# First stage without GpSimd: the initial state on ScalarE, the adding of x on VectorE, operations over two tiles, and a pipeline over pairs

## The chip, the cores and the metric

The kernel runs on one core of one Trainium2 chip. Its metric is the device time of a launch in microseconds. Before the change it is 1729.39 us, the median of 3 runs (1728.51 to 1730.09).

## The reference, cut to what matters

Two recurrent layers work on x of shape 64 x 128 x 512 (batch, time, features), each added to its input. The first is a gated linear recurrence that is written with cumulative sums, so all its time steps can be computed at once; the second is a GRU that goes step by step.

```python
# layer 0: h0 = cond (64, 512)
f  = sigmoid(x @ W_f.T + b_f);  i = sigmoid(x @ W_i.T + b_i)
s  = f + i + EPS
c  = x @ W_h.T + b_h
L  = cumsum(log(f / s + EPS), axis=time)
hidden = cumsum(exp(L_last - L_previous) * (i / s) * c) + exp(L) * h0
x1 = x + hidden
# layer 1: h = 0, video = cond
z = sigmoid(x1[t] @ W_z + h @ U_z + video @ C_z + b_z)
r = sigmoid(x1[t] @ W_r + h @ U_r + video @ C_r + b_r)
hh = tanh(x1[t] @ W + (r * h) @ U + video @ C + b)
h = (1 - z) * h + z * hh;   y[t] = x1[t] + h
```

## The kernel before, in words

The first stage (the span's first 634 us) computes x1, the second (the rest) runs the GRU. Features lie on the 128 partitions, in 4 blocks e.

First stage. The batch is cut into 16 chunks c of 4 rows; a chunk is 512 columns (4 rows x 128 time steps). A tile n is one block e of one chunk, 128 x 512; a pair q is two tiles, and a chunk has two pairs (h = 0 and 1). For each tile TensorE computes three groups (f, i, candidate) of 12 matmuls each (line 717), every group into one of the 8 PSUM banks. Both the weights and x are split into a high and a low part; for the chunk ahead ScalarE writes the high part of x into XS (x_hi, line 318) and VectorE the low one (x_lo, line 489). XS has two slots. The first group of a chunk needs the high part from its first matmul on and the low part from its ninth.

After TensorE, a tile goes back and forth between the engines: sigmoids on ScalarE (lines 344, 349), two gate operations on VectorE (439, 441), two logarithms on ScalarE (354, 355), four scans of 128 steps and an addition on VectorE (470, 475), exp(L) and four exponentials on ScalarE (361, 366), a product and a scan of 512 on VectorE (481, 485). GpSimd multiplies exp(L) with the initial state (826) and adds x (833), and VectorE adds both parts into x1c (459), laid out as (time block, e, time, row). The candidate is multiplied in by VectorE (448). ScalarE loads a table set twice in each pair (351, 369).

SyncE issues the DMAs from its queue. At the start of the pairs with h = 0 it waits until the whole chunk c - 1 is in x1c, stores it into a scratch in DRAM (line 246), and then loads x of chunk c + 1 into the raw buffer that chunk c - 1 has left (line 250). Between the pairs the weights of the second layer come into the buffers called stage; VectorE and ScalarE turn U into two float16 parts in small steps (u_step, 21 of them, and the scalings of line 377), and GpSimd takes three maxima over the partitions (837).

Each engine takes its instructions in the order of its own program; semaphores carry the dependencies. Lines 331 to 378 (ScalarE), 544 to 572 (VectorE), 816 to 837 (GpSimd), 694 to 719 (TensorE, with pair_order) and 241 to 263 (SyncE) set the order of the first stage.

Second stage. 128 steps; in each TensorE works through the recurrent matmuls (761, 773) and 18 projections of the next time block (741). GpSimd takes (1 - z) * h (849), y (860) and the low part of x1 (864), ScalarE its high part (413); the last three read x1 from the raw buffers through a rearranged view.

Of the kernel before, what the change touches and what calls it, by code (L numbers as in the profile page):

```python
# [9 lines left out]
ALU = mybir.AluOpType  # L10
# [21 lines left out]
def build(nc, x, cond, w1, b1, w2, u2, c2, b2, out):  # L32
    ctx = ExitStack()
    with ctx:
# [175 lines left out]
        def last_src(j):  # L210
            return x1c[1][:, j * 128:(j + 1) * 128].rearrange("p (e t b) -> p e t b", e=KT, t=TC)
# [7 lines left out]
        def _(sp):  # L219
# [21 lines left out]
            for q in range(NQ):  # L241
                c, h = divmod(q, 2)
                if h == 0 and c >= 1:

                    sp.wait_ge(s_x1, 4 * c)
                    sp.dma_start(x1d[:, :, c - 1, :].rearrange("j p n -> p j n"),
                                 x1c[(c - 1) % 2].rearrange("p (j n) -> p j n", j=NCH)).then_inc(d_x1d[(c - 1) % 2], 16)
                    if c + 1 < NCH:
                        sp.wait_ge(s_px, 4 * c)
                        sp.dma_start(raw[(c + 1) % 2], x[c + 1]).then_inc(d_x[(c + 1) % 2], 16)  # L250
                if q in (8, 15, 22):
                    g = (8, 15, 22).index(q)
# [13 lines left out]
            sp.wait_ge(s_x1, 4 * NCH)  # L266
# [4 lines left out]
            sp.wait_ge(s_px, 4 * NCH)  # L271
# [29 lines left out]
        def _(act):  # L301
# [29 lines left out]
            for q in range(NQ):  # L331
                c, h = divmod(q, 2)
                if q == NQ - 1:
                    early_hi(0)
                I, G = Ib[q % 2], Gb[q % 2]
                pair = (2 * q, 2 * q + 1)
                for n in pair:
# [561 lines left out]
```

## Time and profile before

| | us |
|---|---|
| median of 3 runs | 1729.39 |
| the profiled execution | 1729.3 |
| its span, first to last instruction | 1727.5 |
| TensorE busy | 1642.9 (95%) |
| VectorE busy | 1516.5 (88%) |
| ScalarE busy | 732.9 (42%) |
| GpSimd busy | 450.6 (26%) |

The mean granted clock of TensorE is 0.980 of full speed. 1.8 us of the profiled execution lie outside the span. The shares are means over both stages; from 700 us on TensorE shows no idle time in the windows, in the first stage it does.

### The profile page before, as it was taken

What the parts mean: (1) busy time and instruction counts of PE and PEld (TensorE: products, weight loads), DVE (VectorE), ACT (ScalarE), POOL (GpSimd) and SP (SyncE); (2) the same over time, 40 slices, a digit from 0 to 9 for tenths busy, and PEclk for the clock granted to TensorE, in tenths of its full rate; (3) what the DMA queues carried; (4) which work ended last, traced back from release to release, by engine and by line L of the source; (5) the groups of instructions that cost most, each with busy time, mean ns of one, the idle gap of its engine ahead of it and who ended that gap; (6) DMA issues with size and microseconds to landing.
All of it is one profiled execution on the core that took longest, in us unless ns stands there. A gap on an engine that the chain in (4) does not pass through costs nothing.

```text
span 1727.5 us, 43869 instructions
## 1 busy us (share of the span) xinstructions
PE 1642.9 (95%) x17918; PEld 1399.7 (81%) x17918; DVE 1516.5 (88%) x3472; ACT 732.9 (42%) x1642; POOL 450.6 (26%) x451
## 2 busy tenths in 40 slices
PE   9988998988999969999999999999999999999997
PEld 6877776767777758888888888888888888888996
DVE  6999989999999986888888888888888888888776
ACT  6656656666667651323322323323323323233222
POOL 1233222332233320222222212222222222222211
PEclk9999998998999989999999999999999999999999
DMA  5111212311211241011011010010010110100000
GB/s 174 50 49 49 73 50 69 102 49 50 73 49 49 74 167 50 2 50 51 2 50 51 2 51 28 25 50 17 36 51 2 51 50 2 51 27 2 27 28 27
DMA packets 45465, 82.51 MB, mean 48 GB/s; under 512 B 1616, under 2 KB 37712, under 8 KB 38480
## 3 DMA queue, kind: packets, MB, share of 16 engines
q1 hardware_dynamic: 45264, 79.71, 13.3%
q8 instruction: 141, 2.31, 0.5%
q14 instruction: 60, 0.49, 0.1%
HBM read 46.15 MB, written 33.55 MB: 46 GB/s over the span
## 4 chain that ended last, share of the span: by engine, by line
PE 65%; DVE 24%; issue 10%; ACT 1%; DMA 0%; DVEq 0%; SPq 0%; POOL 0%; ACTq 0%
PE ps L741 32%; PE ps L773 18%; PE ps L761 12%; DVE Lb L470 8%; DVE AR L481 4%; DVE AR L459 3%; PE ps L717 3%; DVE AR L448 3%; DVE AR L439 2%; DVE AR L485 1%; DVE XS L489 1%; DVE U L517 1%; DVE am L497 0%; DMA raw<-in_x 0%; DVE XS L523 0%
## 5 line engine op out<-in xcount | busy, mean ns | idle before, releaser
L741 PE MATMUL ps<-XS,W 128*128 128x512 f32 (+1 forms) x2448 | 592.6, 388 | 14.7 <-DVE XS L541 14.3
L717 PE MATMUL ps<-XS,W 128*128 128x512 f32 x2304 | 547.9, 400 | 55.9 <-ACT XS L318 49.8
L717 PEld LDWEIGHTS ps<-XS,W 128*128 128x128 f32 x2304 | 443.5, 194 | 160.0 <-issue 57.9
L741 PEld LDWEIGHTS ps<-XS,W 128*128 128x128 f32 x2448 | 426.6, 189 | 85.5 <-issue 15.0
L773 PE MATMUL ps<-HL,U 128*128 128x128 f16 (+1 forms) x4096 | 254.4, 216 | 0.0
L849 POOL TENSOR_TENSOR zc<-zc,Hst 128x256 f32<-128x256 f32 x128 | 94.8, 741 | 586.8 <-ACT zc L399 586.8
L773 PEld LDWEIGHTS ps<-HL,U 128*128 128x128 f16 x4096 | 219.8, 98 | 0.0
L397 ACT ACTIVATE prer<-prer 128x128 f32<-128x128 f32 x256 | 78.5, 310 | 309.4 <-DVE prer L616 270.5
L826 POOL TENSOR_TENSOR AR<-AR,CT 128x512 f32<-128x512 f32 x64 | 83.7, 1308 | 410.6 <-ACT AR L361 410.6
L761 PEld LDWEIGHTS ps<-HL,U 128*128 128x128 f16 x4608 | 152.2, 98 | 35.6 <-issue 34.8
L761 PE MATMUL ps<-HL,U 128*128 128x64 f16 x4608 | 174.8, 193 | 4.9 <-DVE HL L655 4.9
L399 ACT ACTIVATE zc<-prez 128x256 f32<-128x256 f32 x128 | 53.4, 417 | 265.9 <-DVE prez L616 240.0
L592 DVE TENSOR_TENSOR AR<-ps,V 128x512 f32<-128x512 f32 (+1 forms) x204 | 127.7, 652 | 22.8 <-PE ps L741 22.8
L470 DVE TENSOR_TENSOR_SCAN Lb<-AR 128x128 f32<-128x128 f32 x256 | 147.4, 637 | 0.0
L611 DVE SCALAR_TENSOR_TENSOR prer<-ps,du,AR 128x128 f32<-128x128 f32 x256 | 87.5, 347 | 61.0 <-PE ps L773 56.6
L773 PE MATMUL ps<-RL,U 128*128 128x128 f16 (+1 forms) x2048 | 128.7, 216 | 0.5 <-DVE RL L634 0.5
L407 ACT ACTIVATE hn<-Hst 128x256 f32<-128x256 f32 x128 | 53.6, 418 | 143.0 <-DVE Hst L661 143.0
L773 PEld LDWEIGHTS ps<-RL,U 128*128 128x128 f16 x2048 | 110.2, 98 | 1.5 <-DVE RL L634 0.6
L833 POOL TENSOR_TENSOR AR<-AR,raw 128x512 f32<-128x512 f32 x64 | 107.1, 1674 | 6.1 <-POOL AR L826 0.2
L761 PEld LDWEIGHTS ps<-RL,U 128*128 128x128 f16 x2304 | 74.6, 98 | 35.8 <-issue 33.3
L485 DVE TENSOR_TENSOR_SCAN AR<-AR 128x512 f32<-128x512 f32 x64 | 100.6, 1572 | 2.3
L648 DVE SCALAR_TENSOR_TENSOR t<-preh,prez 128x128 f32<-128x128 f32 x256 | 74.2, 295 | 24.4 <-ACT preh L403 24.4
(74 smaller groups left out, 1988.1 us busy)
## 6 DMA issues: line engine op xcount, KB each, us to landing
x_scratch<-AR SPq DMA_DIRECT2D x16, 1024.0 KB, 5.7
raw<-in_x SPq DMA_DIRECT2D x15, 1024.0 KB, 7.8
AR<-x_scratch SPq DMA_DIRECT2D x8, 1024.0 KB, 4.9
out_y<-raw SPq DMA_DIRECT2D x8, 1024.0 KB, 4.5
out_y<-AR SPq DMA_DIRECT2D x7, 1024.0 KB, 4.0
raw<-x_scratch SPq DMA_DIRECT2D x6, 1024.0 KB, 4.8
raw<-x_scratch SPq DMA_DIRECT2D x2, 960.0 KB, 6.4
AR<-in_w1f SPq DMA_DIRECT2D x2, 512.0 KB, 6.3
```

What stands on the lines that cost most here:

```text
L397: act.activation(two(rg, h), two(rg, h), ACT.Sigmoid).then_inc(s_r, 1)
L470: op = dve.tensor_tensor_scan(Lb[:, s * 129 + 1:s * 129 + 129], F[:, z], G[:, z], 0.0, ALU.add, ALU.subtract)
L485: dve.tensor_tensor_scan(g, MK, i, 0.0, ALU.mult, ALU.add).then_inc(s_scanh, 1)
L592: dve.tensor_tensor(XP[j % 2][:, g, e, cols].rearrange("p (t b) -> p t b", b=B), ps[PB[i % 3]][:, 0:n * B].rearrange("p (t b) -> p t b", b=B),
L611: op = dve.scalar_tensor_tensor(out=o, in0=src[:, :, 0:B], scalar=du[:, g:g + 1], in1=xx, op0=ALU.mult, op1=ALU.add)
L717: op = pe.matmul(ps[b][:, :], W[:, wp, g, k, e * P:(e + 1) * P], XS[:, c % 2, xp, k, :], start=n == 0, stop=n == 11)
L741: op = pe.matmul(ps[PB[i % 3]][:, 0:cols.stop - cols.start], W[:, wp, g, k, e * P:(e + 1) * P], XS[:, j % 2, xp, k, cols], start=n == 0, s ...
L761: pe.matmul(ps[b][:, col:col + B], U[:, up, g, k, e * P:(e + 1) * P], S[:, k, 0], start=opens, stop=False, skip_group_check=True)
L773: op = pe.matmul(ps[b][:, col:col + per], U[:, 0, g, k, e * P:(e + 1) * P], S[:, k] if joint else S[:, k, 1], start=False, stop=closes, sk ...
L826: pool.tensor_tensor(v3, v3, h0, ALU.mult).then_inc(s_h0, 1)
L833: pool.tensor_tensor(v, v, raw[c % 2][:, e * 512:(e + 1) * 512], ALU.add).then_inc(s_px, 1)
L849: pool.tensor_tensor(zc, zc, Hst[(t + 1) % 2], ALU.mult).then_inc(s_zch, 1)
```

## The change

The part of each tile that GpSimd did moves: the initial state is multiplied in by ScalarE, as eight copies of 128 columns per pair with a scale for each partition (start_state), and x is added by VectorE (the first operation of finish). Operations from SBUF to SBUF go over both tiles of a pair, 1024 columns. Fb has two buffers. All pairs but the first now have the matmul groups in the order f, i, f, i, candidate, candidate. ScalarE and VectorE work on two pairs at a time: in pair q they do the exponentials, the initial state, the hidden state and finish of pair q - 1. x1 is laid out as (time block, e, row, time), so finish writes runs of 8 elements, and the second stage reads with a step of 8. x_lo moves from the pairs with h = 0 to those with h = 1; x_hi stays in those with h = 0. The loads of the U and C weights come two pairs later. GpSimd keeps the maxima and the second stage.

```diff
-        Fb = AR[:, 4096:5120]
-        Ib = [AR[:, 5120:6144], AR[:, 6144:7168]]
-        Gb = [AR[:, 7168:8192], AR[:, 8192:9216]]
-        Eb = AR[:, 9216:10240]
-        MK = AR[:, 10240:10752]
+        Fb = [AR[:, 4096:5120], AR[:, 5120:6144]]
+        Ib = [AR[:, 6144:7168], AR[:, 7168:8192]]
+        Gb = [AR[:, 8192:9216], AR[:, 9216:10240]]
+        Eb = AR[:, 10240:11264]
+        MK = AR[:, 11264:11776]
...
-            if q == NQ - 1:
-                return ((0, 0), (1, 0), (0, 1), (1, 1), (2, 0), (2, 1))
-            return ((0, 0), (1, 0), (2, 0), (0, 1), (1, 1), (2, 1))
+            return ((0, 0), (1, 0), (0, 1), (1, 1), (2, 0), (2, 1))
...
-            v = raw[j % 4].rearrange("p (c e t b) -> p e t c b", c=NCH, e=KT, t=TC)[:, e]
+            v = raw[j % 4].rearrange("p (c e b t) -> p e t c b", c=NCH, e=KT, t=TC)[:, e]
...
                 if h == 0 and c >= 1:
 
-                    sp.wait_ge(s_x1, 4 * c)
+                    sp.wait_ge(s_x1, 2 * c)
                     sp.dma_start(x1d[:, :, c - 1, :].rearrange("j p n -> p j n"),
                                  x1c[(c - 1) % 2].rearrange("p (j n) -> p j n", j=NCH)).then_inc(d_x1d[(c - 1) % 2], 16)
                     if c + 1 < NCH:
-                        sp.wait_ge(s_px, 4 * c)
+                        sp.wait_ge(s_px, 2 * c)
                         sp.dma_start(raw[(c + 1) % 2], x[c + 1]).then_inc(d_x[(c + 1) % 2], 16)
-                if q in (8, 15, 22):
-                    g = (8, 15, 22).index(q)
+                if q in (10, 17, 24):
+                    g = (10, 17, 24).index(q)
                     sp.wait_ge(s_ulo, KT * (g + 1))
...
+            def sigmoids(q):
+                F, I = Fb[q % 2], Ib[q % 2]
+                for n in (2 * q, 2 * q + 1):
                     e = n % KT
...
+            def logs(q):
+                F, G = Fb[q % 2], Gb[q % 2]
+                act.wait_ge(s_fe, q + 1)
+                act.activation(F, F, ACT.Ln).then_inc(s_lnf, 1)
+                act.activation(G, G, ACT.Ln).then_inc(s_lng, 1)
+
+            def exps(q):
+                G = Gb[q % 2]
+                act.wait_ge(s_scanl, q + 1)
+                if q:
+                    act.wait_ge(s_x1, q)
+                act.activation(Eb.rearrange("p (s t) -> p s t", t=T), Ls[:, :, 1:T + 1], ACT.Exp).then_inc(s_expl, 1)
+                act.wait_ge(s_arg, q + 1)
+                for s in range(8):
+                    z = slice(s * T, (s + 1) * T)
+                    op = act.activation(G[:, z], G[:, z], ACT.Exp, bias=Lb[:, s * 129 + 128:s * 129 + 129], scale=-1.0)
+                    if s % 4 == 3:
+                        op.then_inc(s_exps, 1)
+
+            def start_state(q):
+                c, h = divmod(q, 2)
+                if q == 0:
+                    act.wait_ge(d_cond, 16)
+                act.wait_ge(s_expl, q + 1)
+                for s in range(8):
+                    e, b = 2 * h + s // BC, BC * c + s % BC
+                    z = slice(s * T, (s + 1) * T)
+                    op = act.activation(Eb[:, z], Eb[:, z], ACT.Copy, scale=CT[:, e, b:b + 1])
+                op.then_inc(s_h0, 1)
+
+            for q in range(NQ):
+                c, h = divmod(q, 2)
+                sigmoids(q)
                 act.preload_act_table_set("natural_log_exp_and_others")
...
+                if q:
+                    exps(q - 1)
+                logs(q)
+                if q:
+                    start_state(q - 1)
+                if q < NQ - 1:
+                    act.preload_act_table_set("sigmoid_and_others")
                 if h == 0 and c + 1 < NCH:
                     x_hi(c + 1)
                 i = q - 2
...
                         act.wait_ge(s_uup, g + 1)
                     act.activation(U[:, 0, g, k], stage_at(UZ + g)[:, k * 512:(k + 1) * 512], ACT.Copy,
                                    scale=su[:, g:g + 1]).then_inc(s_uhi, 1)
+            early_hi(0)
+            exps(NQ - 1)
+            start_state(NQ - 1)
+            act.preload_act_table_set("sigmoid_and_others")
...
+            def gates(q):
+                F, I, G = Fb[q % 2], Ib[q % 2], Gb[q % 2]
+                dve.wait_ge(s_sig[0], 2 * q + 2)
+                dve.wait_ge(s_sig[1], 2 * q + 2)
+                if q >= 2:
+                    dve.wait_ge(s_x1, q - 1)
+                dve.scalar_tensor_tensor(out=G, in0=F, scalar=EPS, in1=I, op0=ALU.add, op1=ALU.add).then_inc(s_gs, 1)
+                dve.wait_ge(s_gs, q + 1)
+                dve.scalar_tensor_tensor(out=F, in0=G, scalar=EPS, in1=F, op0=ALU.mult, op1=ALU.add).then_inc(s_fe, 1)
...
+                for s in range(8):
                     z = slice(s * T, (s + 1) * T)
                     op = dve.tensor_tensor_scan(Lb[:, s * 129 + 1:s * 129 + 129], F[:, z], G[:, z], 0.0, ALU.add, ALU.subtract)
-                    if s % 4 == 3:
-                        op.then_inc(s_scanl, 1)
-                gs = G[:, slot(n)].rearrange("p (s t) -> p s t", t=T)
-                dve.wait_ge(s_scanl, n + 1)
-                dve.tensor_tensor(gs, Ls[:, segments(n)[0]:segments(n)[-1] + 1, 0:T], gs, ALU.add).then_inc(s_arg, 1)
...
+            def hidden(q):
+                I, G = Ib[q % 2], Gb[q % 2]
+                dve.wait_ge(s_exps, 2 * q + 2)
+                dve.wait_ge(s_ni, 2 * q + 2)
+                dve.tensor_tensor(I, I, G, ALU.mult).then_inc(s_s, 1)
+                if q == 0:
                     dve.wait_ge(s_mask, 1)
-                dve.wait_ge(s_s, n + 1)
-                dve.tensor_tensor_scan(g, MK, i, 0.0, ALU.mult, ALU.add).then_inc(s_scanh, 1)
...
+            def finish(q):
+                c, h = divmod(q, 2)
+                if c == 0 and h == 0:
+                    dve.wait_ge(d_x0[0], 16)
+                    dve.wait_ge(d_x0[1], 16)
+                if c and h == 0:
+                    dve.wait_ge(d_x[c % 2], 16 * ((c + 1) // 2 if c % 2 else c // 2))
+                dve.wait_ge(s_h0, q + 1)
+                dve.tensor_tensor(Eb, Eb, raw[c % 2][:, h * 1024:(h + 1) * 1024], ALU.add).then_inc(s_px, 1)
+                if h == 0 and c >= 2:
+                    dve.wait_ge(d_x1d[c % 2], 16 * (c // 2))
+                dve.wait_ge(s_scanh, 2 * q + 2)
+                dve.wait_ge(s_px, q + 1)
+                o = x1c[c % 2].rearrange("p (j r t) -> p r j t", j=NCH, t=TC)[:, h * 8:(h + 1) * 8]
+                g, v = (w.rearrange("p (r j t) -> p r j t", r=8, j=NCH) for w in (Gb[q % 2], Eb))
+                dve.tensor_tensor(o, g, v, ALU.add).then_inc(s_x1, 1)
...
+                gates(q)
+                candidate(2 * q)
+                if h == 1 and c + 1 < NCH:
+                    x_lo(c + 1)
+                if 0 <= q - 2 < 21 and (q - 2) % 7 < 3:
+                    u_step(q - 2)
+                if 0 <= q - 3 < 21 and (q - 3) % 7 >= 3:
+                    u_step(q - 3)
                 if q:
-                    x1_tile(n0 - 2)
-                    x1_tile(n0 - 1)
-                gates(n1)
-                if not late:
-                    candidate(n1)
-                scan_logs(n0)
-                scan_logs(n1)
-                if late:
-                    candidate(n0)
-                    candidate(n1)
-                hidden(n0)
-                hidden(n1)
-                if h == 0 and c + 1 < NCH:
-                    x_lo(c + 1)
-                if 0 <= q - 2 < 21:
-                    u_step(q - 2)
-            x1_tile(4 * NCH - 2)
-            x1_tile(4 * NCH - 1)
+                    hidden(q - 1)
+                scan_logs(q)
+                candidate(2 * q + 1)
+                if q:
+                    finish(q - 1)
+            early_lo(0)
+            hidden(NQ - 1)
+            finish(NQ - 1)
...
-                for n in (2 * q, 2 * q + 1):
-                    e = n % KT
-                    v = Eb[:, slot(n)]
-                    v3 = v.rearrange("p (b t) -> p b t", b=BC)
-                    h0 = CT[:, e, BC * c:BC * (c + 1)].unsqueeze(2).to_broadcast([P, BC, T])
-                    pool.wait_ge(s_expl, n + 1)
-                    pool.tensor_tensor(v3, v3, h0, ALU.mult).then_inc(s_h0, 1)
-                    if c and e == 0:
-                        pool.wait_ge(d_x[c % 2], 16 * ((c + 1) // 2 if c % 2 else c // 2))
-                    if c == 0 and e == 0:
-                        pool.wait_ge(d_x0[0], 16)
-                        pool.wait_ge(d_x0[1], 16)
-                    pool.wait_ge(s_h0, n + 1)
-                    pool.tensor_tensor(v, v, raw[c % 2][:, e * 512:(e + 1) * 512], ALU.add).then_inc(s_px, 1)
...
```

VectorE, after, from the second half of pair 2 (chunk 1, h = 0) to the beginning of pair 3. AR holds F, I, G, E and x1c, Lb the scanned logarithms.

```order
L481 SCALAR_TENSOR_TENSOR Lb<-AR 128x128 [waits ln_g]
L481 SCALAR_TENSOR_TENSOR Lb<-AR 128x128 x7
L485 TENSOR_TENSOR AR<-Lb,AR 128x1024 [waits scan_l]
L471 SCALAR_TENSOR_TENSOR AR<-ps,B,AR 128x512 [waits mm2]
L506 TENSOR_TENSOR AR<-AR,raw 128x1024 [waits h0]
L513 TENSOR_TENSOR AR<-AR 128x8x16x8 [waits plus_x,scan_h]
L462 SCALAR_TENSOR_TENSOR AR<-AR 128x1024 [waits x1,sig_i,sig_f]
L464 SCALAR_TENSOR_TENSOR AR<-AR 128x1024 [waits gs]
L471 SCALAR_TENSOR_TENSOR AR<-ps,B,AR 128x512 [waits mm2]
L517 TENSOR_TENSOR XS<-raw,XS 128x2048 [waits xhi]
```

The same engine before, at the beginning of pair 2.

```order
L439 SCALAR_TENSOR_TENSOR AR<-AR 128x512 [waits sig_i,sig_f]
L441 SCALAR_TENSOR_TENSOR AR<-AR 128x512 [waits gs]
L448 SCALAR_TENSOR_TENSOR AR<-ps,B,AR 128x512 [waits mm2]
L459 TENSOR_TENSOR AR<-AR 128x4x16x8 [waits scan_h,plus_x] x2
L439 SCALAR_TENSOR_TENSOR AR<-AR 128x512 [waits sig_i,sig_f]
L441 SCALAR_TENSOR_TENSOR AR<-AR 128x512 [waits gs]
L448 SCALAR_TENSOR_TENSOR AR<-ps,B,AR 128x512 [waits mm2]
L470 SCALAR_TENSOR_TENSOR Lb<-AR 128x128 [waits exp_s,ln_g]
```

The completion of the pair before stood as the fourth row of a pair (L459, 4 * c tiles then complete for SyncE's store and load); now it stands at the very end of the pair (L506, L513), and the scans of the pair itself stand ahead of it.

ScalarE before, in pair 2, from its second logarithms to the sigmoids of pair 3.

```order
L354 ACTIVATE AR<-AR 128x512 [waits fe]
L355 ACTIVATE AR<-AR 128x512
L361 ACTIVATE AR<-Lb 128x512 [waits x1,scan_l]
L366 ACTIVATE AR<-AR,Lb 128x128 [waits arg]
L366 ACTIVATE AR<-AR,Lb 128x128 x3
L361 ACTIVATE AR<-Lb 128x512 [waits x1,scan_l]
L366 ACTIVATE AR<-AR,Lb 128x128 [waits arg]
L366 ACTIVATE AR<-AR,Lb 128x128 x3
L369 ACT_TABLE_LOAD
L318 ACTIVATE XS<-raw 128x2048 [waits mm2,d_x_0]
L344 ACTIVATE AR<-ps,B 128x512 [waits scan_l,mm0]
L349 ACTIVATE AR<-ps,B 128x512 [waits scan_h,mm1]
```

ScalarE after, in pair 2, from its first table load to the sigmoids of pair 3. The semaphore d_x_0 is that of x's loads into raw buffer 0; in pair 2 it is the load of chunk 2.

```order
L379 ACT_TABLE_LOAD
L357 ACTIVATE AR<-Lb 128x1024 [waits x1,scan_l]
L361 ACTIVATE AR<-AR,Lb 128x128 [waits arg]
L361 ACTIVATE AR<-AR,Lb 128x128 x7
L349 ACTIVATE AR<-AR 128x1024 [waits fe]
L350 ACTIVATE AR<-AR 128x1024
L373 ACTIVATE AR<-AR,CT 128x128 [waits exp_l]
L373 ACTIVATE AR<-AR,CT 128x128 x7
L386 ACT_TABLE_LOAD
L316 ACTIVATE XS<-raw 128x2048 [waits mm2,d_x_0]
L338 ACTIVATE AR<-ps,B 128x512 [waits scan_l,mm0]
L343 ACTIVATE AR<-ps,B 128x512 [waits scan_h,mm1]
```

The copy of x into XS (L318, now L316) is still the last thing ahead of the next pair's sigmoids and still waits for the load, while the exponentials ahead of it now belong to the pair before. SyncE's own order of the store and this load is as it was; its waits count pairs instead of tiles.

## Rows read from the trace of the kernel before

**Rows 1.** Windows: stretch, length, busy time of each engine, TensorE clock, DMA share, GB/s.

```profile
50.00:100.00 50.00, 49.90 (x220) 41.00 (x219) 49.45 (x59) 32.79 (x57) 17.41 (x12) 1.00 0.14 43
114.00:118.00 4.00, 4.00 (x11) 2.77 (x11) 2.85 (x3) 3.28 (x5) 0.00 (x0) 0.57 0.02 4
```

**Rows 2.** Waits of 0 to 640 us: total, times, longest us.

```profile
PE ps L717 <- ACT XS L318: 49.8, 13, 8.3
```

**Rows 3.** Timeline, VectorE, two stretches of pairs: start, us, instruction.

```profile
310.31 1.22 DVE L485 TENSOR_TENSOR_SCAN AR<-AR 128x512 f32<-128x512 f32 x1
311.46 2.27 DVE L489 TENSOR_TENSOR XS<-raw,XS 128x2048 fp32r<-128x2048 f32 x1
...
314.30 0.68 DVE L439 SCALAR_TENSOR_TENSOR AR<-AR 128x512 f32<-128x512 f32 x1
315.02 0.69 DVE L441 SCALAR_TENSOR_TENSOR AR<-AR 128x512 f32<-128x512 f32 x1
315.63 0.74 DVE L448 SCALAR_TENSOR_TENSOR AR<-ps,B,AR 128x512 f32<-128x512 f32 x1
316.29 1.97 DVE L459 TENSOR_TENSOR AR<-AR 128x512 f32<-128x512 f32 x2
...
320.08 1.36 DVE L470 TENSOR_TENSOR_SCAN Lb<-AR 128x128 f32<-128x128 f32 x4
321.48 0.69 DVE L475 TENSOR_TENSOR AR<-Lb,AR 128x512 f32<-128x512 f32 x1
322.09 3.21 DVE L470 TENSOR_TENSOR_SCAN Lb<-AR 128x128 f32<-128x128 f32 x4
```

**Rows 4.** Timeline of the same stretch: SyncE's queue and ScalarE.

```profile
298.28 0.38 SPq L246 DMA_DIRECT2D x_scratch<-AR  x1
298.70 1.79 SPq L250 DMA_DIRECT2D raw<-in_x  x1
...
302.20 1.28 ACT L366 ACTIVATE AR<-AR,Lb 128x128 f32<-128x128 f32 x4
...
308.71 1.91 ACT L318 ACTIVATE XS<-raw 128x2048 fp32r<-128x2048 f32 x1
310.53 0.71 ACT L377 ACTIVATE U<-AR,su 128x512 f16<-128x512 f32 x1
311.14 0.67 ACT L344 ACTIVATE AR<-ps,B 128x512 f32<-128x512 f32 x1
...
313.56 1.28 ACT L351 ACT_TABLE_LOAD   x1
...
315.74 0.63 ACT L354 ACTIVATE AR<-AR 128x512 f32<-128x512 f32 x1 [0.90 <-DVE AR L441]
316.28 0.62 ACT L355 ACTIVATE AR<-AR 128x512 f32<-128x512 f32 x1
```

**Rows 5.** DMA issues of the page: count, KB each, median us to landing.

```profile
raw<-in_x SPq DMA_DIRECT2D x15, 1024.0 KB, 7.8
```

**Rows 6.** Timeline: pair 0's last sigmoid, the gates of pairs 2 and 30, the last x1.

```profile
21.84 0.69 ACT L349 ACTIVATE AR<-ps,B 128x512 f32<-128x512 f32 x1 [1.09 <-PE ps L717]
...
58.61 0.67 DVE L439 SCALAR_TENSOR_TENSOR AR<-AR 128x512 f32<-128x512 f32 x1
...
595.39 0.67 DVE L439 SCALAR_TENSOR_TENSOR AR<-AR 128x512 f32<-128x512 f32 x1
...
632.03 1.90 DVE L459 TENSOR_TENSOR AR<-AR 128x512 f32<-128x512 f32 x2
```

**Rows 7.** Groups by line of 0 to 640 us: busy, mean ns, idle before.

```profile
L459 DVE TENSOR_TENSOR AR<-AR 128x512 f32<-128x512 f32 x64 | 63.4, 1074 | 0.0
```

**Rows 8.** The same view of 800 to 1200 us.

```profile
L860 POOL TENSOR_TENSOR AR<-AR,hn 128x256 f32<-128x256 f32 x31 | 22.7, 732 | 61.4 <-ACT hn L407 61.4
L413 ACT ACTIVATE XS<-raw 128x512 fp32r<-128x512 f32 x16 | 9.8, 615 | 0.0
```

**Rows 9.** Waits of 800 to 1200 us: total, times, longest us.

```profile
POOL zc L849 <- ACT zc L399: 205.6, 48, 4.9
```

More of the change, by code:

```diff
@@ L329, in w2_hi @@
                 act.activation(W[:, 0, g], stage_k(W2_STAGE[g]), ACT.Copy).then_inc(s_w2hi, 1)
[L331 to L337, printed above, removed]
+            def sigmoids(q):
+                F, I = Fb[q % 2], Ib[q % 2]
+                for n in (2 * q, 2 * q + 1):
                     e = n % KT
-                    if q == 0 and n == 0:
+                    if n == 0:
                         act.wait_ge(d_b1, 16)
                     act.wait_ge(s_mm[0], n + 1)
-                    if q:
-                        act.wait_ge(s_scanl, n - 1)
-                    act.activation(Fb[:, slot(n)], ps[bank(0, n)][:, :], ACT.Sigmoid,
+                    if q >= 2:
+                        act.wait_ge(s_scanl, q - 1)
+                    act.activation(F[:, slot(n)], ps[bank(0, n)][:, :], ACT.Sigmoid,
                                    bias=B1[:, 0, e:e + 1]).then_inc(s_sig[0], 1)
@@ L449, in candidate @@
                                          op0=ALU.add, op1=ALU.mult).then_inc(s_ni, 1)
-            def x1_tile(n):
-                c, e = divmod(n, KT)
-                o = x1c[c % 2].rearrange("p (j e t b) -> p e b j t", j=NCH, e=KT, t=TC)[:, e]
-                g, v = (w[:, slot(n)].rearrange("p (b j t) -> p b j t", b=BC, j=NCH) for w in (Gb[n // 2 % 2], Eb))
-                dve.wait_ge(s_px, n + 1)
-                if e == 0 and c >= 2:
-                    dve.wait_ge(d_x1d[c % 2], 16 * (c // 2))
-                dve.wait_ge(s_scanh, n + 1)
-                dve.tensor_tensor(o, g, v, ALU.add).then_inc(s_x1, 1)
@@ L461, in scan_logs @@
-            def scan_logs(n):
-                if n == 0:
-                    dve.wait_ge(s_lzero, 1)
-                dve.wait_ge(s_lng, n + 1)
-                if n >= 2:
-                    dve.wait_ge(s_exps, n - 1)
-                F, G = Fb, Gb[n // 2 % 2]
-                for s in segments(n):
+            def scan_logs(q):
+                F, G = Fb[q % 2], Gb[q % 2]
+                if q == 0:
+                    dve.wait_ge(s_lzero, 1)
+                dve.wait_ge(s_lng, q + 1)
+                for s in range(8):
@@ L477, in hidden @@
[L477 to L485 removed]
+                op.then_inc(s_scanl, 1)
@@ new lines, in scan_logs @@
+                g8 = G.rearrange("p (s t) -> p s t", t=T)
+                dve.wait_ge(s_scanl, q + 1)
+                dve.tensor_tensor(g8, Ls[:, :, 0:T], g8, ALU.add).then_inc(s_arg, 1)
+            def hidden(q):
[3 more added lines that the diff above has]
+                dve.tensor_tensor(I, I, G, ALU.mult).then_inc(s_s, 1)
+                if q == 0:
+                    dve.wait_ge(s_mask, 1)
+                dve.wait_ge(s_s, q + 1)
+                for n in (2 * q, 2 * q + 1):
+                    dve.tensor_tensor_scan(G[:, slot(n)], MK, I[:, slot(n)], 0.0, ALU.mult, ALU.add).then_inc(s_scanh, 1)
@@ L545, in _ @@
                 c, h = divmod(q, 2)
[L546 to L549 removed]
+                if q == NQ - 1:
                     add_b2(1)
[L551 to L572 removed]
+                gates(q)
[6 more added lines that the diff above has]
+                    u_step(q - 3)
+                if q:
+                    hidden(q - 1)
[6 more added lines that the diff above has]
+            finish(NQ - 1)
             last_lo(0)
@@ L895 @@
     y = np.asarray(r.results[0]["out_y"])
-    first = y[:-1].reshape(NCH - 1, P, NCH, KT, TC, BC).transpose(2, 5, 0, 4, 3, 1).reshape(B, T - TC, KT * P)
+    first = y[:-1].reshape(NCH - 1, P, NCH, KT, BC, TC).transpose(2, 4, 0, 5, 3, 1).reshape(B, T - TC, KT * P)
     last = y[-1].reshape(P, TC, KT, B).transpose(3, 1, 2, 0).reshape(B, TC, KT * P)
```

66 lines of the change are left out of this document (12 added, 54 removed).

## The prediction

> **What bounds the kernel now.** I read the windows first, then the waits of the first stage, then its timeline pair by pair. In the first stage VectorE works without a break: 49.45 of 50 us, while TensorE does 220 matmuls in 49.90 us, 0.2268 us each at the full clock, as long as it is fed [rows 1]. The waits show that it isn't always: 13 times TensorE stood before a chunk's first group until ScalarE had copied x into XS, 49.8 us in all [rows 2]. From the gates of pair 2 (58.61) to those of pair 30 (595.39) 28 pairs take 536.8 us, 19.2 each [rows 6], and 72 matmuls would take 72 x 0.2268 = 16.3. VectorE sets the pace, and part of its time isn't its own: four scans of 128 take 1.36 us at 320.08 and 3.21 us at 322.09 [rows 3], while GpSimd multiplies and adds.
>
> The second stage hardly changes; the question is what a chunk (two pairs) takes in the first.
>
> **The change, engine by engine.** Durations are start to start where the next row allows it. On VectorE a further 512 columns cost (2.27 - 0.69) / 3 = 0.53 us, on ScalarE (1.91 - 0.62) / 3 = 0.43 [rows 3, 4].
>
> VectorE, per pair: gates 0.72 + 0.53 = 1.25 and 0.61 + 0.53 = 1.14; two candidates of 0.66; hidden 1.25 for the product and 2 x 1.15 for the scans = 3.55; eight scans at the undisturbed pace 2 x 1.40 - 0.1 = 2.7, and their addition 0.61 + 0.53 = 1.14, together 3.84; finish 1.25 + 1.22 = 2.47 [rows 3]. That is 13.6, and 2.2 for x_lo in every second pair: 14.7 a pair instead of 19.2. Adding x costs VectorE 1.25 more; the undisturbed scans, the wide operations and the last addition (two of 512 took 1.97 with a step of four elements in what they write; I take 1.22 for 1024 in runs of 8, with 1.97 as the other end [rows 3]) give back more.
>
> ScalarE, per pair: four sigmoids 2.42, two table loads 2.56, exponentials 0.63 + 0.43 + 2 x 1.28 = 3.6, logarithms 0.97 + 1.06 = 2.03, the eight copies for the initial state 2.5 and half of an x_hi (1.82) [rows 4]. No row shows such a copy; the nearest are the exponentials of 128 with an operand for each partition, four in 1.28, so 2.5, with 2.0 and 3.5 as ends. Sum 14.0. GpSimd: nothing is left of its two operations.
>
> Both are below TensorE's 16.3, so by throughput the stage would be bound by the matmuls. But the engines wait for each other in order, and there the change puts one thing badly.
>
> **The load of x moves behind the end of the pair.** SyncE may load x of chunk c + 1 only when chunk c - 1 is finished, since it goes into the same buffer. Before, that was complete at the fourth operation of pair 2c; ScalarE came to x_hi ten us later (the load issued at 298.70, the copy at 308.71 [rows 4]) and a load lands in 7.8 [rows 5]: hidden, with 2 us to spare. Now finish(2c - 1) is VectorE's last operation of pair 2c, and x_hi(c + 1) is still in ScalarE's part of that same pair, ahead of the sigmoids of pair 2c + 1, which all later work needs. Counted from the end of pair 2c's sigmoids:
>
> - ScalarE: table 1.28, exponentials to 4.9, logarithms to 6.9, initial state to 9.4, table to 10.7. It stands at x_hi from 10.7 on.
> - VectorE: gates and a candidate to 3.1, waits for the exponentials at 4.9; hidden 3.55, scans 3.84, candidate 0.66, finish 2.47: 15.4.
> - The queue: 0.03 to the store, 0.42 to the load behind it (298.28 to 298.70), 7.8 to landing [rows 4, 5]: 23.65.
> - x_hi 1.82, sigmoids of pair 2c + 1 2.42 [rows 4]: 27.9.
>
> So ScalarE waits 13 us in each pair with h = 0 of chunks 1 to 14, and everything behind it on its queue with it; VectorE runs dry at 15.4. TensorE, which has eight banks of lead, ends its chunk and then waits as well.
>
> Pair 2c + 1, again from its sigmoids: VectorE would take 1.25 + 1.14 + 0.66 + 2.18 (x_lo) + 3.55 + 3.84 + 0.66 + 2.47 = 15.75. TensorE, though, needs the low part of x, there at 3.05 + 2.27 = 5.3, for the ninth matmul of the next chunk, and from it 4 + 36 matmuls to the last group that the sigmoids of the next pair want: 40 x 0.2268 = 9.1, and 0.7 for the sigmoid: 15.1. Behind an idle time of some us the clock is lower: in 114 to 118 us, at 0.57 of full speed on average (the 1.2 GHz level for most of it), just behind such a wait, 11 matmuls ran where 17.6 fit [rows 1], 1.5 us lost. Here it idles about 4.5 us for the high part and 5.8 for the low one in each chunk, so I add 1.5: 16.6. TensorE then decides this pair by 0.9.
>
> **The sum.** A chunk takes 27.9 + 16.6 = 44.5; 14 chunks (pairs 2 to 29) 623. Six scalings of U (0.61 each, 310.53 to 311.14 [rows 4]) stand behind x_hi: 3.7. For the 21 small steps on VectorE, most of which lie under its wait for the exponentials, I take 4 (between 0 and 12). So 631 against 536.8: +94. Before that, pair 1 gets its sigmoids earlier: pair 0's end at 22.5 [rows 6] stays; h, h and four more groups later (6 x 2.72 = 16.3) pair 1 has its gates at 38.9, pair 2 at 55.2 instead of 58.6: -3.4. From the gates of pair 30 to the last x1: one pair at TensorE's pace 16.3, the path of pair 31 15.4, and the part that now trails, exponentials 3.6, hidden 3.55 and finish 2.47, 9.6: 41.3 against 632.03 + 1.90 - 595.39 = 38.5 [rows 6]: +2.8. Total +93.6 on a span of 1727.5, 1821.1; with the 1.8 around it 1822.9. The median of the runs is 0.1 above the profiled execution, so I forecast 1823.
>
> **The second stage.** x1 is now read with a step of 8 elements where before four lay together: y on GpSimd (732 ns) and the low part (line 864), and the high part on ScalarE (615 ns) [rows 8]. The only row on a step is line 459, whose writes had a step of four: 1074 ns instead of the 690 of its neighbours [rows 3, 7], 0.38 for 512. For 127 y of 256 and 56 + 56 conversions of 512 that would be 24 + 43 = 67 us on two engines. I cost it at nothing: GpSimd waits 205.6 us in 48 steps for ScalarE, 4.3 in each [rows 9], and TensorE is the engine without gaps there. If the cover weren't there, the price is up to those 67.
>
> The Trainium skill, page SBUF — State Buffer, section "Door 1: The DMA port swizzle", says that SBUF has lines of 16 bytes, that accesses within one run at full rate, and that each change of line costs. For the first stage it speaks for the new layout (runs of 32 bytes written in place of single elements), and the 1074 ns of line 459 agree [rows 7]. For the second it speaks against it: each element read there lies in a line of its own. By it the 67 us are incurred on those engines, though not on the path.
>
> **The rivals.**
> - The same wait, but no lower clock on the path: TensorE has idle stretches before each chunk in the trace too. Then VectorE's 15.75 decides the second pair, the first, with ScalarE's table load 0.65 behind, takes 14.8 + 8.25 + 4.24 = 27.3; 43.0 a chunk, 1802.
> - **Faster:** the stage runs at TensorE's pace, x_hi never holds anything up. It would take x in the buffer when ScalarE comes, 10.7 into the pair. 28 pairs x 16.3 = 457 instead of 536.8, -3.4 and +2.8: -80, 1649. For it: VectorE 14.7 and ScalarE 14.0 are both below 16.3. Against it: the program orders finish(2c - 1) ahead of the load and the load ahead of the sigmoids, and 15.4 + 8.25 is 13 after 10.7. It turns at a chunk of 38.3; even the first rival is 4.7 above that.
> - The second stage pays for the step: the forecast and up to 67, 1823 to 1890, if GpSimd's longer reads hold up VectorE's, which take the two inputs the long scans took.
>
> **How the numbers follow.** Forecast 0.80, first rival 0.09, faster 0.04, second stage 0.05, and 0.02 that it lies near no change because the pieces are far shorter than their rows. The likeliest time is 1823. Its terms reach from 1802 (the clock costs nothing) to 1840 (finish at 1.97 adds 0.75 to the first pair of a chunk, 14 x 0.75 = 10, and the small steps 8 more); with part of the second stage's price 1848. Range 1800 to 1848. A measurement of this kernel tells 0.2% from no change. Faster 0.04, same 0.01, slower 0.95.
>
> **What would show it.** In the new profile: waits of ScalarE's copy (L316) for the load of x, 14 times 12 to 14 us, some 180 in all; waits of VectorE's gates for the sigmoids; chunks of 44 to 45 us from gates to gates, in turns of 28 and 16.6; VectorE's scans of 128 all at the pace of the four in 1.36 us; GpSimd idle in the stage; the clock at its lower level behind each chunk's start; the last x1 near 727 us. If ScalarE doesn't wait for the load, the forecast is wrong at its core. If it does and the chunk takes 43, the clock term is. If the time from the last x1 to the end grows by more than 5 us, the second stage's is.

## The result, and the profile after

The change makes the kernel 6.3% slower: 1838.39 us, median of 4 runs (1836.24 to 1840.26), against 1729.73 of the kernel before; ratio 1.0629, 95% interval 1.0611 to 1.0648. The forecast was 1823, range 1800 to 1848. The profiled execution took 1836.24 us, its span 1834.4, 106.9 more than before; the mean granted clock is 0.952.

The page after: span, busy time of the engines, and the chain that ended last by engine.

```profile
span 1834.4 us, 43572 instructions
...
PE 1674.8 (91%) x17918; PEld 1420.1 (77%) x17918; DVE 1405.4 (77%) x3344; ACT 819.4 (45%) x1802; POOL 295.6 (16%) x323
...
PE 70%; DVE 14%; DMA 6%; ACT 6%; issue 3%; SPq 0%; DVEq 0%; ACTq 0%
```

VectorE has 111 us less work and GpSimd 155, and the kernel takes 107 more. DMA now holds 6% of the chain of work that ended last. The waits of the first stage (0 to 760 us) say which transfer; each line has the total, the number and the longest in us:

```profile
DVE AR L462 <- ACT AR L343: 209.7, 30, 13.5
ACT XS L316 <- DMA raw<-in_x: 187.2, 14, 13.8
...
PE ps L737 <- ACT XS L316: 65.1, 14, 5.1
PE ps L737 <- DVE XS L517: 60.9, 14, 4.7
ACT AR L343 <- PE ps L737: 44.5, 28, 2.0
...
DVE AR L491 <- ACT AR L361: 13.8, 13, 1.5
```

ScalarE's copy of x into XS, which never waited for its load before, now waits 14 times, 13.4 us each. VectorE's gates wait for the sigmoids behind that copy, and TensorE waits twice per chunk, for the high part (65.1 where it was 49.8 [rows 2]) and for the low one (60.9 where it was 3.5).

One chunk in order of time, SyncE and ScalarE, the counterpart of [rows 4]:

```profile
299.61 0.38 SPq L244 DMA_DIRECT2D x_scratch<-AR  x1
300.03 1.84 SPq L248 DMA_DIRECT2D raw<-in_x  x1
...
307.80 1.91 ACT L316 ACTIVATE XS<-raw 128x2048 fp32r<-128x2048 f32 x1 [13.22 <-DMA raw<-in_x]
309.62 0.71 ACT L394 ACTIVATE U<-AR,su 128x512 f16<-128x512 f32 x1
310.23 0.67 ACT L338 ACTIVATE AR<-ps,B 128x512 f32<-128x512 f32 x1
...
311.94 0.69 ACT L343 ACTIVATE AR<-ps,B 128x512 f32<-128x512 f32 x1
312.65 1.28 ACT L379 ACT_TABLE_LOAD   x1
313.94 1.06 ACT L357 ACTIVATE AR<-Lb 128x1024 f32<-128x1024 f32 x1
314.91 2.43 ACT L361 ACTIVATE AR<-AR,Lb 128x128 f32<-128x128 f32 x8
```

ScalarE stood at its copy from 294.6 on, but the load left the queue at 300.03 and landed 7.8 us later. Before, the load left ten us ahead of the copy. VectorE in the pair that follows, the counterpart of [rows 3]:

```profile
312.73 1.23 DVE L462 SCALAR_TENSOR_TENSOR AR<-AR 128x1024 f32<-128x1024 f32 x1 [13.15 <-ACT AR L343]
313.99 1.22 DVE L464 SCALAR_TENSOR_TENSOR AR<-AR 128x1024 f32<-128x1024 f32 x1
...
318.66 1.22 DVE L491 TENSOR_TENSOR AR<-AR 128x1024 f32<-128x1024 f32 x1
319.91 2.34 DVE L496 TENSOR_TENSOR_SCAN AR<-AR 128x512 f32<-128x512 f32 x2
322.16 2.60 DVE L481 TENSOR_TENSOR_SCAN Lb<-AR 128x128 f32<-128x128 f32 x8
324.80 1.22 DVE L485 TENSOR_TENSOR AR<-Lb,AR 128x1024 f32<-128x1024 f32 x1
...
326.61 1.22 DVE L506 TENSOR_TENSOR AR<-AR,raw 128x1024 f32<-128x1024 f32 x1
327.96 1.23 DVE L513 TENSOR_TENSOR AR<-AR 128x1024 f32<-128x1024 f32 x1
329.93 1.23 DVE L462 SCALAR_TENSOR_TENSOR AR<-AR 128x1024 f32<-128x1024 f32 x1 [0.75 <-ACT AR L343]
```

Everything after the 13 us of idle time goes as planned: eight scans in 2.60, no long one among them, the last addition in 1.23. The pair takes 312.73 to 329.93, 17.2, and even then VectorE ends by waiting 0.75.

The 28 pairs from 55.88 to 695.18 take 639.3 us (536.8 before [rows 6]): the 14 with h = 0 28.1 each, those with h = 1 17.6. A chunk takes 45.7, a little over the 44 to 45 that were to show it. The last x1 is there at 739.86 instead of 633.93, +105.9; the second stage grew by 1.0.

### The profile page after: what moved, and what is told of

Its sections match the earlier page's. It is cut to its first block, busy times and chain, and to the rows that moved or that the text cites. A ratio compares the mean times of both kernels' runs of the same rounds, so it can differ in the third digit from the quotient of the medians.

```text
span 1834.4 us, 43572 instructions
## 1 busy us (share of the span) xinstructions
PE 1674.8 (91%) x17918; PEld 1420.1 (77%) x17918; DVE 1405.4 (77%) x3344; ACT 819.4 (45%) x1802; POOL 295.6 (16%) x323
## 4 chain that ended last, share of the span: by engine, by line
PE 70%; DVE 14%; DMA 6%; ACT 6%; issue 3%; SPq 0%; DVEq 0%; ACTq 0%
PE ps L761 30%; PE ps L793 17%; PE ps L737 11%; PE ps L781 11%; DMA raw<-in_x 6%; DVE Lb L481 2%; DVE AR L496 2%; DVE XS L517 2%; ACT AR L361 2%; DVE AR L471 1%; DVE AR L491 1%; DVE AR L513 1%; DVE AR L462 1%; DVE AR L506 1%; ACT AR L343 1%
## 5 line engine op out<-in xcount | busy, mean ns | idle before, releaser
L737 PE MATMUL ps<-XS,W 128*128 128x512 f32 x2304 | 581.0, 416 | 129.6 <-ACT XS L316 65.1
L737 PEld LDWEIGHTS ps<-XS,W 128*128 128x128 f32 x2304 | 464.6, 203 | 245.7 <-issue 73.3
L761 PEld LDWEIGHTS ps<-XS,W 128*128 128x128 f32 x2448 | 426.1, 189 | 86.4 <-issue 16.1
L462 DVE SCALAR_TENSOR_TENSOR AR<-AR 128x1024 f32<-128x1024 f32 x32 | 39.2, 1225 | 213.9 <-ACT AR L343 209.7
L316 ACT ACTIVATE XS<-raw 128x2048 fp32r<-128x2048 f32 x15 | 28.6, 1910 | 187.2 <-DMA raw<-in_x 187.2
L424 ACT ACTIVATE preh<-preh 128x128 f32<-128x128 f32 x256 | 77.5, 309 | 37.4 <-DVE preh L636 37.4
L781 PE MATMUL ps<-RL,U 128*128 128x64 f16 x2304 | 89.4, 193 | 2.3 <-DVE RL L650 2.3
```

The source lines that it names most:

```text
L424: act.activation(two(hg, h), two(hg, h), ACT.Tanh).then_inc(s_hh, 1)
L462: dve.scalar_tensor_tensor(out=G, in0=F, scalar=EPS, in1=I, op0=ALU.add, op1=ALU.add).then_inc(s_gs, 1)
L737: op = pe.matmul(ps[b][:, :], W[:, wp, g, k, e * P:(e + 1) * P], XS[:, c % 2, xp, k, :], start=n == 0, stop=n == 11)
L761: op = pe.matmul(ps[PB[i % 3]][:, 0:cols.stop - cols.start], W[:, wp, g, k, e * P:(e + 1) * P], XS[:, j % 2, xp, k, cols], start=n == 0, s ...
L781: pe.matmul(ps[b][:, col:col + B], U[:, up, g, k, e * P:(e + 1) * P], S[:, k, 0], start=opens, stop=False, skip_group_check=True)
```

## The experiments

Each was timed beside the kernel before on the same chip. Ratios are to that kernel; differences are to the changed kernel's 1838.4 unless said otherwise.

### x loaded for two chunks only

```diff
                     if c + 1 < NCH:
                         sp.wait_ge(s_px, 2 * c)
-                        sp.dma_start(raw[(c + 1) % 2], x[c + 1]).then_inc(d_x[(c + 1) % 2], 16)
```

The waits of ScalarE and VectorE for the loads that are left out go with them.

> The changed kernel with x loaded for chunks 0 and 1 only; later chunks use what lies in the two buffers, so they compute on other data and the 14 later loads are left out. Theory (the wait for the load of x is the whole loss): no wait at the copy of x is left, the stage runs at TensorE's pace, 28 pairs at 16.3 to 16.6 us instead of 22.8, and the kernel takes 1650 to 1665 us, about 175 less than the changed kernel's 1838. Rival (the chain between the engines over two pairs, or TensorE's clock, sets the pace and the load only fills its slack): a chunk stays above 38 us, the time above 1730.

Measured: 1654.2 us, ratio 0.9560 (0.9546 to 0.9574), 184 less. A window of 480 us in its first stage (columns as in [rows 1]):

```profile
60.00:540.00 480.00, 480.00 (x2156) 398.80 (x2155) 438.91 (x581) 407.08 (x761) 1.08 (x3) 1.00 0.15 46
```

TensorE never stops and its clock is full. With x in place the changed pipeline runs at TensorE's pace, 16.3 us a pair; the rival falls.

The control, the same taken out of the kernel before:

> Control for the run with x loaded for two chunks only: the same taken from the kernel before (later chunks compute on what lies in the buffers). Theory: there the load was hidden, so leaving the 14 loads out changes nothing: 1730, within 4 us. Rival (the loads cost through traffic in the DMA engines or SBUF, whatever waits for them): several tens of us less.

Measured: 1729.05, ratio 0.9995 (0.9985 to 1.0004). In the kernel before the transfers cost nothing by themselves. For the changed pipeline the run with all three changes of order, below, says the same: it has all the loads and takes 1.1 us more than the run without them. What costs is the wait that the change made.

### The load ahead of the store

```diff
-                    sp.wait_ge(s_x1, 2 * c)
-                    sp.dma_start(x1d..., x1c[(c - 1) % 2]...)
                     if c + 1 < NCH:
                         sp.wait_ge(s_px, 2 * c)
                         sp.dma_start(raw[(c + 1) % 2], x[c + 1])...
+                    sp.wait_ge(s_x1, 2 * c)
+                    sp.dma_start(x1d..., x1c[(c - 1) % 2]...)
```

> The changed kernel with SyncE's load of x ahead of the store of x1, waiting for the adding of x alone. Theory: the load is issued 1.25 (last addition) + 0.42 (store's issue) earlier, 14 x 1.7 = 23 us, and lands sooner as well with no megabyte ahead of it in the DMA engines: a lone megabyte of the stage lands 4.8 to 5.0 us after its issue, so up to 3 us more per chunk, 64 us in all. 1774 to 1815, most likely 1780. Rival (the load isn't the bound): within 5 us of 1838.

Measured: 1776.98, ratio 1.0270 (1.0255 to 1.0285), 61.4 less, 4.4 per chunk. Issues on its page: count, KB, us to landing.

```profile
raw<-in_x SPq DMA_DIRECT2D x15, 1024.0 KB, 5.3
```

Landing fell from 7.8 [rows 5] to 5.3, and ScalarE's wait from 187.2 to 128.3 us. Landing 2.5 us sooner and leaving 1.7 sooner (the load leaves 1.2 us after the adding of x begins, where it was 3.0) make the 4.2 us by which each of these waits is shorter. The sooner landing comes with the changed order; how the two transfers share the DMA engines no row shows.

### finish ahead of the scans

```diff
                     hidden(q - 1)
+                    finish(q - 1)
                 scan_logs(q)
                 candidate(2 * q + 1)
-                if q:
-                    finish(q - 1)
```

(and on ScalarE start_state(q - 1) ahead of logs(q)).

> The changed kernel with finish(q - 1) straight behind hidden(q - 1) on VectorE, ahead of the scans of pair q, and the initial state ahead of the logarithms on ScalarE. Theory: the last x1 of a chunk, and with it the load, comes 3.84 + 0.66 = 4.5 us earlier in the pair: 14 x 4.5 = 63 less, 1775. The logarithms come 2.4 later, which VectorE doesn't notice (finish lies ahead). Rival: VectorE's work per pair is the same, so if its chain were the bound the time stays within 5 us of 1838.

Measured: 1777.25, ratio 1.0268 (1.0251 to 1.0285), 61.1 less. Not an instruction was added or taken away; the wait for the load is 128.0 us.

### Both

> The changed kernel with both: the load of x ahead of the store, and finish ahead of the scans. Theory: the load is issued at 9.7 of the pair with h = 0 and lands at 14.7; ScalarE stands at the copy from 10.7, so 4 of the 13 us of waiting remain, a chunk takes 19 + 17.6 = 36.6 instead of 45.8: 129 less, 1710. Rival (the two gains are the same one): 1777, as each alone.

Measured: 1704.72, ratio 0.9853 (0.9839 to 0.9868), 133.7 less, 11 us over the sum of the two (122.5). ScalarE's wait for the load is down to 68.4 us, by the sum of what each edit took off (118.8 against 58.9 + 59.2), so the surplus lies elsewhere: the larger part in the pairs with h = 1, which take 16.9 instead of 17.5 and 17.6, while TensorE's wait for the low part falls to 31.9 us (81.8 and 81.7 in the two runs). Whether that is its clock no run separates. This is already faster than the kernel before.

### The copy of x moved to the pairs with h = 1

```diff
                 sigmoids(q)
                 act.preload_act_table_set("natural_log_exp_and_others")
+                if h == 1 and c + 1 < NCH:
+                    x_hi(c + 1)
                 if q:
                     exps(q - 1)
...
-                if h == 0 and c + 1 < NCH:
-                    x_hi(c + 1)
```

> The changed kernel with ScalarE's copy of x (x_hi) behind the sigmoids and the table load of the pairs with h = 1 instead of at the end of those with h = 0. Theory: the load takes as long as before, but the gates of pair 2c + 1 no longer wait for it; the exponentials do. A chunk then takes about 23.65 (landing) + 1.9 + 3.6 + 3.55 + 3.84 + 0.66 + 2.47 = 39.6 by its chain, and TensorE, fed at 27.8, wants 39.1: 40.5 with the same excess as seen, so 14 x 5.2 = 73 less, 1765. Rival (order on ScalarE doesn't matter, the load's latency alone does): 1838, since the load is issued at the same place.

Measured: 1755.10, ratio 1.0146 (1.0131 to 1.0161), 83.3 less. Its waits in the first stage:

```profile
ACT XS L316 <- DMA raw<-in_x: 86.4, 14, 6.9
DVE XS L517 <- ACT XS L316: 86.4, 14, 6.9
...
PE ps L737 <- ACT XS L316: 67.4, 14, 5.5
```

The load is issued as late as in the changed kernel; what changed is what stands behind the engine that waits for it. The pairs take 16.1 (h = 0) and 23.7 (h = 1), 39.8 together (expected 40.5).

### All three

> All three: load ahead of the store, finish ahead of the scans, copy of x behind the sigmoids of the pairs with h = 1. Theory: x has landed (14.7) before ScalarE comes to the copy (about 16 to 17), no engine waits for the load; the pairs take 15.4 and about 17 by VectorE's chain against 16.3 by TensorE, so the stage runs at TensorE's pace within a few us: 1655 to 1675, near the run without the loads (1654), and faster than the kernel before. Rival (the copy in the way of the exponentials makes VectorE wait): pairs of 19 us with h = 1, 1700.

Measured: 1655.30 (1654.21 to 1656.29), ratio 0.9567 (0.9553 to 0.9582): 4.3% faster than the kernel before, and within 1.1 us of the run without the loads. The same window as above:

```profile
60.00:540.00 480.00, 480.00 (x2141) 398.22 (x2140) 440.05 (x579) 407.19 (x763) 1.08 (x3) 1.00 0.24 77
```

No wait for the load is left; the first stage is TensorE's. Pairs take 15.7 (h = 0) and 17.0 (h = 1), 16.3 on average. The instructions are those of the changed kernel; only their order differs.

### One part alone: GpSimd's two operations moved, nothing else

```diff
+                    for s in seg:
+                        z = slice(s * T, (s + 1) * T)
+                        b = BC * c + s % BC
+                        op = act.activation(Eb[:, z], Eb[:, z], ACT.Copy, scale=CT[:, n % KT, b:b + 1])
+                    op.then_inc(s_h0, 1)
...
+                dve.wait_ge(s_h0, n + 1)
+                dve.tensor_tensor(Eb[:, slot(n)], Eb[:, slot(n)], raw[c % 2][:, e * 512:(e + 1) * 512],
+                                  ALU.add).then_inc(s_px, 1)
```

in the order, widths and layout of the kernel before.

> The kernel before with one part of the change alone: the initial state by four copies of 128 columns per tile on ScalarE, x added by VectorE in 512 columns ahead of x1_tile, GpSimd without work in the first stage; order, layout and widths as before. Theory (GpSimd's reads lengthened VectorE's scans and products): per pair VectorE gains 3.21 - 1.36 and about 1.7 at the scan of 512 and the product, and pays 2 x 0.7 for x and 0.7 for a wait for ScalarE's later exponentials: 1.5 less a pair, 42 in all, 1688. Scans of 128 at 0.4 us. Rival (the long scans are their own or another engine's doing): no scan gets shorter, and the added work makes it 1.4 a pair slower, 1770.

Measured: 1731.82, ratio 1.0010 (1.0001 to 1.0020): no gain, where 42 us were expected. Its groups by line (lines 486, 501, 497 are 470, 485, 481 of before):

```profile
L486 DVE TENSOR_TENSOR_SCAN Lb<-AR 128x128 f32<-128x128 f32 x256 | 87.2, 404 | 0.0
L501 DVE TENSOR_TENSOR_SCAN AR<-AR 128x512 f32<-128x512 f32 x64 | 78.4, 1224 | 2.3
...
L497 DVE TENSOR_TENSOR AR<-AR 128x512 f32<-128x512 f32 x64 | 44.0, 688 | 10.6 <-ACT AR L366 10.6
L447 DVE SCALAR_TENSOR_TENSOR AR<-AR 128x512 f32<-128x512 f32 x64 | 43.8, 684 | 17.3 <-ACT AR L349 17.3
L469 DVE TENSOR_TENSOR AR<-AR,raw 128x512 f32<-128x512 f32 x64 | 43.5, 680 | 0.0
...
L505 DVE TENSOR_TENSOR XS<-raw,XS 128x2048 fp32r<-128x2048 f32 x15 | 34.4, 2292 | 36.6 <-ACT XS L318 36.6
L533 DVE SCALAR_TENSOR_TENSOR U<-AR,su,U 128x512 f16<-128x512 f32 x12 | 9.0, 748 | 7.7 <-ACT U L385 7.7
```

The expected gain on VectorE came: the scans of 128 took 147.4 us before and take 87.2, those of 512 went from 100.6 to 78.4, the products from 76.4 to 44.0, 115 us of VectorE in all, and adding x costs 43.5. But the other 72 come back as waits of VectorE for ScalarE, which now has eight more copies per pair (2.5 us) inside the same round trip: 36.6 for the copy of x, 17.3 for sigmoids, 10.6 for exponentials, 7.7 for the scalings. With the pipeline over pairs and x in time the same work keeps to TensorE's 16.3 us a pair, as the run with all three changes of order shows.

### One part alone: the layout of x1

```diff
-                o = x1c[c % 2].rearrange("p (j e t b) -> p e b j t", ...)
+                o = x1c[c % 2].rearrange("p (j e b t) -> p e b j t", ...)
```

and every reader of it.

> The kernel before with the new layout of x1 alone: line 459 writes runs of 8 elements (step of 128 between them) instead of single elements with a step of 4, and the second stage reads with a step of 8. Theory: the writes cost the 0.38 us that line 459 takes more than its neighbours; with runs it takes 0.69 like them, 0.3 per tile start to start on an engine that sets the pace, 64 x 0.3 = 19 less, and the second stage is covered, + 1: 1712. Rival (its four-dimensional reading pattern is what costs, or VectorE isn't the bound of the first stage): 1730.

Measured: 1713.27, ratio 0.9911 (0.9897 to 0.9924), 15.6 less than the kernel before beside it (1728.82).

```profile
L459 DVE TENSOR_TENSOR AR<-AR 128x512 f32<-128x512 f32 x64 | 41.0, 681 | 0.0
```

681 ns where it was 1074 [rows 7]: the step of four in the writes was the cost, not the pattern of the reads, which is as before. The last x1 comes 19.3 us earlier, as expected; the second stage takes 1.8 longer where 1 was put.

### Matmuls that fill TensorE's waits

```diff
+                    if first:
+                        for _ in range(16):
+                            pe.matmul(ps[b][:, :], W[:, 0, 0, 0, 0:P], W[:, 0, 0, 0, :], start=True, stop=True)
                     for n in range(12):
+                        if first and n == 2 * KT:
+                            ...  # 16 more, into the next group's bank
```

(first: the first group of chunks 1 to 15).

> The changed kernel with 16 matmuls of 512 columns that nobody uses on TensorE while it waits for the high part of x of each chunk, and 16 while it waits for the low part (2 x 3.6 us at the full clock, inside waits of 4.5 us each), so that its clock stays up. Theory (the excess of the pairs with h = 1, 17.5 us against VectorE's 15.75, is the lower clock behind the waits): these pairs take 16.0 to 16.4, 14 x 1.3 = 18 less, 1820; the load's wait stays at 187 us. Rival (the excess is latency between engines, or the fillers come at the low clock and run over): the same within 3 us, or a few us slower.

Measured: 1834.01, ratio 1.0602 (1.0587 to 1.0618), 4.4 less by the medians and 2.3 by the profiled spans. The interval overlaps that of the changed kernel (1.0611 to 1.0648), so the net gain is hardly told from none; what the run teaches is in its pairs. Here 318.49 to 335.09 is the pair that was 312.73 to 329.93, 16.6 us. The window that holds both waits of that chunk:

```profile
312.00:326.00 14.00, 10.47 (x45) 8.03 (x44) 7.44 (x7) 12.41 (x22) 0.00 (x0) 1.00 0.06 26
```

The same two waits in the changed kernel, from the end of one chunk's matmuls to the low part of x:

```profile
306.00:318.00 12.00, 3.75 (x8) 2.48 (x8) 5.24 (x5) 10.17 (x17) 0.00 (x0) 0.58 0.10 40
```

The clock stays up in this chunk, but not in all: in the 3 us behind the low part it is 1.00 in seven of the 14 chunks and between 0.50 and 0.75 in the other seven, for instance here, behind a wait of 2.6 us:

```profile
187.00:190.00 3.00, 3.00 (x8) 2.35 (x8) 2.97 (x4) 3.00 (x9) 0.00 (x0) 0.50 0.02 5
```

The pairs with h = 1 take 16.8 instead of 17.6 on average, 11 us in 14 chunks (7 of them in the seven chunks where the clock held); those with h = 0 stay at 28.2 (28.1). Chunk 1, where there was no wait to fill, gave back 7.3 (the pair ahead of it, held up by the fillers, took 23.6 instead of 16.3), which explains the small net. Where the clock held and no small step stands on VectorE (four pairs), the pair takes 15.93, and VectorE goes from its last operation to the next pair's gates without waiting, as at the end of the one from 588.65 to 604.57:

```profile
603.20 1.23 DVE L513 TENSOR_TENSOR AR<-AR 128x1024 f32<-128x1024 f32 x1
604.57 1.23 DVE L462 SCALAR_TENSOR_TENSOR AR<-AR 128x1024 f32<-128x1024 f32 x1
```

The same four take 17.0 to 18.3 in the changed kernel. So the lower clock costs the changed kernel at least 11 us of its 107. For the seven chunks whose clock fell, an estimate from VectorE's rows (15.93 for a pair, and 0.67 more where a scaling stands in it) gives some 7.5 us in place of the 4 measured, so the whole would be near 15. The 0.8 us per chunk that came back are less than the 1.3 expected, because the fillers held the clock in half of the chunks only and the small steps on VectorE then set the pair.

## Why the prediction was right

**The load behind the end of the pair.** Right in place and nearly in size. ScalarE's wait was forecast at 14 times 12 to 14 us, some 180; it is 14 times, 187.2. The pair with h = 0 was put at 27.9 plus a scaling in six of them; it takes 28.1. Taking the loads out gives 184 us back, and each of three edits that touch only when the load is issued, lands or is waited for gives 61 to 83. The order of instructions alone made a change with 111 us less work on VectorE slower by 107.

**The pair with h = 1.** The term that was mis-sized: 16.6 forecast, 16.9 with the 4 us allowed for small steps, 17.6 measured, 10 us in all. It was put together as TensorE's 5.3 + 9.1 + 1.5 + 0.7. The low part of x came as forecast (318.13, 5.4 after the gates), and TensorE's waits were 4.7 and 4.4 us where 4.5 and 5.8 were put. The 1.5 for the clock was too little, because the time at the lower level differs from chunk to chunk. The first 5.4 us behind the low part in two chunks, one whose pair took 18.2 and the one shown above, 17.2:

```profile
271.60:277.00 5.40, 5.39 (x13) 4.23 (x14) 4.78 (x12) 5.37 (x12) 0.35 (x1) 0.50 0.00 0
318.10:323.50 5.40, 5.37 (x16) 4.31 (x17) 5.37 (x9) 5.37 (x12) 0.00 (x0) 0.67 0.00 0
```

At 0.50 of full speed (1.2 GHz throughout) 13 matmuls ran, at 0.67 16, where 5.4 / 0.2268 = 24 fit: 2.5 and 1.8 us lost instead of 1.5. Where the fillers held the clock and no small step was in the way, the pair fell to VectorE's own 15.93 (15.75 forecast), so the other terms of the sum stand. The pairs with h = 0 came out 1.4 us under their sum, which hides a little of the miss, so the 28 pairs take 639.3 against 631, +8.3.

**The end of the stage.** 41.3 forecast, 739.86 - 695.18 = 44.7. The 32 matmuls of the conditioning ahead of the last pair's groups were left out: 3.68 us on TensorE, and the pair from gates to gates takes 19.94 where 16.3 was put. Before, that pair took 20.3 (595.39 to 615.64), hardly more than the 19.2 of VectorE's pace, so they barely showed; when the bound moves to another engine, everything on that engine has to be counted again.

**The start** of the stage: 55.2 forecast, 55.88. **The second stage:** nothing forecast, +1.0 measured (+1.8 with the layout alone), though part of its cover was used. The readers after, in 900 to 1300 us:

```profile
L861 POOL TENSOR_TENSOR AR<-AR,hn 128x256 f32<-128x256 f32 x30 | 26.4, 881 | 58.9 <-ACT hn L428 58.9
L865 POOL TENSOR_TENSOR XS<-raw,XS 128x512 fp32r<-128x512 f32 x16 | 24.5, 1531 | 2.5 <-ACT XS L434 1.8
L434 ACT ACTIVATE XS<-raw 128x512 fp32r<-128x512 f32 x16 | 18.2, 1139 | 0.0
```

881 ns instead of 732, and 1139 instead of 615 [rows 8]: all pay for the step of 8, and GpSimd still waits 188 us for ScalarE in 48 steps (205.6 before [rows 9]). Summed, +8.3, +0.7, +3.4 and +1.0 are 13.4, and the span exceeds the forecast's 1821.1 by 13.3; the other 2 us of the miss are the median, which lies 2.2 above the profiled execution where 0.1 was put.

**The rivals.** The one without a clock term (1802) falls: the second pair takes 17.6 in the changed kernel, and comes near this rival's 15.75 only where the fillers held the clock. The faster one (1649) named what the design can do: once x is in the buffer in time, 1654 and 1655 were measured. It needed three changes of order that the change doesn't make. The widths, the pipeline and the undisturbed VectorE did what they were costed at: eight scans 2.60 (2.7 put), finish 1.22 + 1.23, the eight copies of the initial state 2.43 (2.5 put).

The rule on lines of 16 bytes from the Trainium skill, page SBUF — State Buffer, section "Door 1: The DMA port swizzle", holds on both sides here: writes of single elements cost 1074 ns and runs 681; reads whose elements each lie in another line cost ScalarE 1139 ns instead of 615.

Open: what decides whether the clock falls behind a wait. With the same fillers it held in seven chunks and fell in seven, and no run separates them.

## What to carry to other kernels

When a step is moved to the end of a loop body, look at what its completion releases: here a buffer, and through it a load whose reader stood early on another engine's queue. Add up release, queue, landing and reader (15.4 + 8.25 us), and compare with when the reader gets there (10.7); if it is late, move the release forward, the load ahead of other transfers, or the reader back, each of which paid 61 to 83 us here and together 183. When work is taken off the busiest engine, ask whether the engine that takes it is in the same round trip: the part with GpSimd's operations alone freed 115 us on VectorE, brought 43.5 of new work and 72 of waits, and gained nothing.

## What the runs showed that was not expected

A megabyte loaded right behind a store of a megabyte lands in 7.8 us, ahead of it in 5.3. Filling TensorE's waits of some 4.5 us with 16 matmuls each kept the granted clock at 1.00 in only seven of 14 chunks. Copying 512 columns with a step of 8 elements in what is read costs ScalarE 0.52 us more (1139 against 615 ns), GpSimd's subtraction, whose other operands have no step, 0.26 (1531 against 1268 ns). I had put 0.38 on both from VectorE's writes.
